# Adding a bias row to 100,000 node rows beside a sort: on GpSimd, or in 128 pieces on TensorE and ScalarE

## The reference

```python
edge_index = jnp.stack([src, dst])
h = jnp.maximum(_layernorm(x, axis=-1), 0.0)
x = x + _L0_gnn_ref(h, edge_index, L0_gnn_W, L0_gnn_att_src, L0_gnn_att_dst, L0_gnn_bias)
# ... and the same with _L1_gnn_ref, _L2_gnn_ref, _L3_gnn_ref

# inside _L0_gnn_ref
out = jax.ops.segment_sum(alpha[:, None] * h[src], dst, num_segments=N_NODES)
return jnp.tanh(out + bias)
```

## Time and profile before

| | us |
|---|---|
| three timed runs, median (lowest to highest) | 8423.18 (8384.15 to 8427.1) |
| span of the profiled execution, the only time given of it | 8526.1 |
| start of the stage with sort and node pass in that span | 42.7 |
| last instruction of the sort's network ends | 574.5 |
| last addition of the node pass ends | 709.2 |
| first instruction of layer 0 | 736.6 |

### The profile page before, as it was taken

One profiled execution on the slowest core, in us unless ns is written; L12 is line 12 of the kernel. 1 busy time (PEld: TensorE's weight loads), 2 busy tenths in 40 slices (PEclk: granted clock), 3 DMA queues, 4 the chain that ended last, 5 costly groups with the idle time before them and its releaser, 6 DMA issues. The chain is left out here.

```text
span 8526.1 us, 74303 instructions
## 1 busy us (share of the span) xinstructions
PE 4101.6 (48%) x11974; PEld 2134.1 (25%) x11974; DVE 5430.6 (64%) x9130; ACT 2417.4 (28%) x4857; POOL 5497.4 (64%) x5789
## 2 busy tenths in 40 slices
PE   0002444444466666400056666666577776666620
PEld 0000111111122222100033333433344433333310
DVE  6854777777577777699246666666544445555554
ACT  1111333333333333333023333333222222222210
POOL 5775666666566666588767777777544446666645
PEclk9999999999766666655555555555578777777765
DMA  2332222222333333377211111111122221222248
GB/s 83 98 98 74 63 63 63 64 65 57 98 93 93 93 93 93 101 216 212 51 34 40 39 41 39 40 40 39 39 62 61 62 53 40 41 40 40 41 126 249
DMA packets 846528, 647.53 MB, mean 76 GB/s; under 512 B 656112, under 2 KB 684269, under 8 KB 846271
## 3 DMA queue, kind: packets, MB, share of 16 engines
q1 hardware_dynamic: 691399, 463.53, 19.2%
q0 software_dynamic: 150560, 157.85, 8.8%
q10 hardware_dynamic: 4512, 25.60, 1.0%
HBM read 385.69 MB, written 274.56 MB: 77 GB/s over the span
## 5 line engine op out<-in xcount | busy, mean ns | idle before, releaser
L729 POOL DMA_INDIRECT l_rows<-x,l_num x1176 | 1186.5, 1009 | 461.0 <-issue 376.9
L754 POOL DMA_INDIRECT o<-l_out,l_snum x392 | 412.9, 1053 | 370.0 <-DVEq L1245 245.9
L1348 POOL DMA_INDIRECT er_edge_rows<-eat,all_perm x392 | 532.4, 1358 | 144.7 <-issue 133.8
L754 POOL DMA_INDIRECT x<-l_out,l_snum x392 | 411.3, 1049 | 305.7 <-DVEq L1095 199.6
L754 POOL DMA_INDIRECT xh<-l_out,l_snum x392 | 407.8, 1040 | 248.0 <-issue 149.5
L729 POOL DMA_INDIRECT l_rows<-in_x,l_num x392 | 444.4, 1134 | 170.4 <-issue 124.3
L754 POOL DMA_INDIRECT g<-l3b_out,l3b_snum x392 | 396.8, 1012 | 203.9 <-issue 158.1
L729 POOL DMA_INDIRECT l3b_rows<-g_rows,l3b_num x392 | 386.8, 987 | 170.8 <-issue 142.7
L729 POOL DMA_INDIRECT l3a_rows<-xh,l3a_num x392 | 383.3, 978 | 171.4 <-issue 96.9
L682 ACT ACTIVATE l_ex<-l_ex 128x1024 f32<-128x1024 f32 x294 | 310.6, 1056 | 603.5 <-DVEq L678 420.3
L949 POOL DMA_INDIRECT pre_src_rows<-in_x,all_idx_src x392 | 387.2, 988 | 141.6 <-issue 126.8
(11 more groups left out here) (368 smaller groups left out, 12553.8 us busy)
## 6 DMA issues: line engine op xcount, KB each, us to landing
l_far<-far_d SPq DMA_DIRECT2D x196, 256.0 KB
x<-ts_row SPq DMA_DIRECT2D x31, 812.5 KB
d_xrow<-x SPq DMA_DIRECT2D x31, 812.5 KB
l_far<-far_s SPq DMA_DIRECT2D x98, 256.0 KB
o<-l_fill_o SPq DMA_DIRECT2D x97, 256.0 KB
g<-l_fill SPq DMA_DIRECT2D x97, 256.0 KB
xh<-l_fill_h SPq DMA_DIRECT2D x97, 256.0 KB
ts_xin<-in_x SPq DMA_DIRECT2D x31, 800.0 KB
```

The lines of the kernel that those rows point to most:

```text
L729: pool.indirect_dma_start(self.buf[k.u][:, j, at:at + w], None, table, bass.IndirectOffsetOnAxis(ap=self.num[k.u][:, m, j:j + 1], axis=0)) ...
L754: pool.indirect_dma_start(self.table, bass.IndirectOffsetOnAxis(ap=self.num[k.u][:, j:j + 1], axis=0), self.out[k.u][:, j, 0:self.cols], N ...
L1348: pool.indirect_dma_start(c.edge_rows[:, t, :], None, eat, bass.IndirectOffsetOnAxis(ap=c.perm[:, t:t + 1], axis=0)).then_inc(c.edges_gath ...
```

## The change

GpSimd no longer adds anything. Each chunk of the node pass is cut into four pieces of 7, 6, 6 and 6 rows (448 or 384 columns), 128 pieces in all. For a piece TensorE multiplies the piece by the identity into a PSUM bank and adds, by a second product of a row of ones with the bias's tanh (now one partition of 7 copies), the bias to it. ScalarE copies the sum from PSUM to the output tile. Piece number m stands right behind level m of the sort in the streams of TensorE (behind the flip of that level, if it has one) and of ScalarE (behind the payload copy). Two PSUM banks alternate, so TensorE may be two pieces ahead of ScalarE. TensorE now waits for a chunk's load, and ScalarE for the store that frees its output buffer. SyncE's waits count pieces instead of chunks. SyncE stores the marks `far_d` and `keep_d` ahead of the node pass, for which it waits until VectorE has made them. GpSimd's stream is left with the fills and the 392 gathers.

```diff
-                beside_sync(sp)
-
                 sp.wait_ge(to_store, 1)
                 sp.dma_start(dram["far_d"].rearrange("(b p f) -> p b f", p=P, f=P), start[:]).then_inc(stored, 16)
                 sp.dma_start(dram["keep_d"].rearrange("(b p f) -> p b f", p=P, f=P), flag[:]).then_inc(stored, 16)
+
+                beside_sync(sp)
...
                     act.activation(pay[(n + 1) % 2][:], pay[n % 2][:], ACT.Copy).then_inc(pay_copied, 1)
+                    row_piece_act(act, n)
...
                         layout = need
+                    row_piece_pe(pe, m)
...
+ROW_PIECES = ((0, 7), (7, 13), (13, 19), (19, NR))
...
-    s.tb = s.sb("tb", [P, D])
+    s.tb = s.sb("tb", [1, 7, D])
+    s.p_row = [s.ps(f"p_row{u}", (P, 7 * D)) for u in range(2)]
...
+    def piece_pe(pe, m):
...
+        k = Chunk(m // per // 2, m // per % 2, c.NODE_CH)
+        lo, hi = ROW_PIECES[m % per]
+        at = s.p_row[m % 2][:, 0:(hi - lo) * D]
+        if m % per == 0:
+            pe.wait_ge(s.xin_loaded[k.u], 16 * (k.t + 1))
+        if m >= 2:
+            pe.wait_ge(s.piece_done, m - 1)
+        pe.matmul(at, c.ident[:], s.xin[k.u][:, lo:hi, :].rearrange("p r f -> p (r f)"), start=True, stop=False)
+        pe.matmul(at, c.ones_row[:], s.tb[:, 0:hi - lo, :].rearrange("p r f -> p (r f)"), start=False, stop=True).then_inc(s.piece_added, 1)
+
+    def piece_act(act, m):
...
+        if m % per == 0 and not k.first:
+            act.wait_ge(s.stored[k.u], 16 * k.t)
+        act.wait_ge(s.piece_added, m + 1)
+        act.activation(s.row[k.u][:, lo:hi, POS:POS + D], s.p_row[m % 2][:, 0:(hi - lo) * D].rearrange("p (r f) -> p r f", f=D),
+                       ACT.Copy).then_inc(s.piece_done, 1)
...
-                    sp.wait_ge(s.row_done, k.n - 2)
+                    sp.wait_ge(s.piece_done, per * (k.n - 2))
...
-        for i in range(c.NODE_CH):
...
-            pool.tensor_tensor(s.row[k.u][:, :, POS:POS + D], s.xin[k.u][:], over_rows(s.tb[0:NP, :], NR),
-                               ALU.add).then_inc(s.row_done, 1)
-            if i == 0:
-                hold(pool, c.src_known, 1)
-            for t in range(i * per, min(c.NT, (i + 1) * per)):
-                pool.indirect_dma_start(c.src_rows[:, t, :], None, x, bass.IndirectOffsetOnAxis(ap=c.idx_src[:, t:t + 1], axis=0)
-                                        ).then_inc(c.src_gathered, 16)
+        hold(pool, c.src_known, 1)
+        for t in range(c.NT):
+            pool.indirect_dma_start(c.src_rows[:, t, :], None, x, bass.IndirectOffsetOnAxis(ap=c.idx_src[:, t:t + 1], axis=0)
+                                    ).then_inc(c.src_gathered, 16)
```

More of the change, by code:

```diff
@@ L164, in prep_lists @@
     N = c.N
-    beside_act, beside_sync, beside_pool = beside
+    beside_act, beside_sync, beside_pool, row_piece_pe, row_piece_act = beside
     full, rest = E // P, E % P
@@ L905, in tables_start @@
     s.row = [s.sb(f"row{u}", [NP, NR, POS + D]) for u in range(2)]
-    s.tb = s.sb("tb", [P, D])
+    s.tb = s.sb("tb", [1, 7, D])
+    s.p_row = [s.ps(f"p_row{u}", (P, 7 * D)) for u in range(2)]
     s.xin_loaded = [s.sem(f"xin_loaded{u}") for u in range(2)]
     s.stored = [s.sem(f"stored{u}") for u in range(2)]
-    s.row_done, s.tanh_done, s.zeroed, s.ends, s.no_pos = (s.sem(n) for n in ("row_done", "tanh_done", "zeroed", "ends", "no_pos"))
+    s.piece_done, s.piece_added, s.tanh_done, s.zeroed, s.ends, s.no_pos = (
+        s.sem(n) for n in ("piece_done", "piece_added", "tanh_done", "zeroed", "ends", "no_pos"))
+    per = len(ROW_PIECES)
+    pieces = c.NODE_CH * per
     def scalar(act):
-        act.activation(s.tb[:], c.bias0[:], ACT.Tanh).then_inc(s.tanh_done, 1)
+        act.activation(s.tb[:], over_rows(c.bias0[0:1, :], 7), ACT.Tanh).then_inc(s.tanh_done, 1)
+        act.wait_ge(s.no_pos, 3)
+    def piece_pe(pe, m):
+        if m >= pieces:
+            return
+        if m == 0:
+            pe.wait_ge(s.tanh_done, 1)
+        k = Chunk(m // per // 2, m // per % 2, c.NODE_CH)
[8 more added lines that the diff above has]
+    def piece_act(act, m):
+        if m >= pieces:
+            return
+        k = Chunk(m // per // 2, m // per % 2, c.NODE_CH)
+        lo, hi = ROW_PIECES[m % per]
+        if m % per == 0 and not k.first:
[3 more added lines that the diff above has]
+                       ACT.Copy).then_inc(s.piece_done, 1)
     def sync(sp):
@@ L920, in body @@
                 if not k.first:
-                    sp.wait_ge(s.row_done, k.n - 2)
+                    sp.wait_ge(s.piece_done, per * (k.n - 2))
                 sp.dma_start(s.xin[k.u][0:node_parts(c, k)], node_rows(c, x, k)).then_inc(s.xin_loaded[k.u], 16)
             if old:
-                sp.wait_ge(s.row_done, old.n)
+                sp.wait_ge(s.piece_done, per * old.n)
                 sp.dma_start(node_rows(c, tab1, old), s.row[old.u][0:node_parts(c, old)]).then_inc(s.stored[old.u], 16)
@@ L935, in gpsimd @@
         pool.iota(c.pos[:], pattern=[[P, c.NT]], base=0, channel_multiplier=1).then_inc(s.no_pos, 1)
-        pool.wait_ge(s.no_pos, 3)
-        pool.wait_ge(s.tanh_done, 1)
-        t, per = 0, -(-c.NT // c.NODE_CH)
-        for i in range(c.NODE_CH):
[L940 to L943, removed]
-            pool.tensor_tensor(s.row[k.u][:, :, POS:POS + D], s.xin[k.u][:], over_rows(s.tb[0:NP, :], NR),
-                               ALU.add).then_inc(s.row_done, 1)
-            if i == 0:
-                hold(pool, c.src_known, 1)
-            for t in range(i * per, min(c.NT, (i + 1) * per)):
-                pool.indirect_dma_start(c.src_rows[:, t, :], None, x, bass.IndirectOffsetOnAxis(ap=c.idx_src[:, t:t + 1], axis=0)
-                                        ).then_inc(c.src_gathered, 16)
-    return scalar, sync, gpsimd
+        hold(pool, c.src_known, 1)
+        for t in range(c.NT):
+            pool.indirect_dma_start(c.src_rows[:, t, :], None, x, bass.IndirectOffsetOnAxis(ap=c.idx_src[:, t:t + 1], axis=0)
+                                    ).then_inc(c.src_gathered, 16)
+    return scalar, sync, gpsimd, piece_pe, piece_act
 class Fill:
```

## The result

| | before | after |
|---|---|---|
| timed, median (lowest to highest) | 8423.19 us (8384.15 to 8427.1, 4 runs) | 8275.98 us (8258.88 to 8300.62, 4 runs) |
| ratio of the times, 95% interval | | 0.9842 (0.981 to 0.9873) |
| span of the profiled execution | 8526.1 us | 8258.0 us |
| first and last gather start | 83.7, 704.6 | 80.5, 597.7 |
| last level of the sort starts | 572.0 | 530.5 |

The kernel became faster by 147 us of median; the forecast was a gain of 135 us, to 8288. Layer 0 starts 131 us sooner. The timeline at the end of the new first stage answers to the earlier trace rows. A row gives start and duration in us, engine, line and operation, and in brackets the idle time before it and what ended it.

The account below looks back on a forecast made before the run. The first stage was taken as bound by GpSimd's stream of gathers and additions; without additions the train ends at 599.4, plus 2.5 layer 0 starts at 602, not 736.6: gain 135 us, 8288 us, range 8250 to 8345.

Parts of the forecast that it names:

- GpSimd's additions, 103 us: GpSimd's gather train: removing 30 additions inside it, 3.44 us each, cuts it from 620.9 to 518 us.
- VectorE's stalls, 82 us, and the bare sort: Sort on VectorE: 23 stalls beside GpSimd's additions vanish, 82 us; the sort then takes 395 us and ends at 489.
- The wait of 140 us: VectorE behind the sort: its 140 us idle time goes, since the marks are stored before the node pass.
- queues passed: SyncE's queue: the sorted keys' store stays behind the node pass, which ends with level 127 of 136, so free.
- Which end is later: End of the first stage: GpSimd's gathers put layer 0 at 602, the sort would allow 511; GpSimd's is later.
- The barrier, 2.5 us: Before layer 0: 2.5 us added to the gathers' end at 599.4, so layer 0 starts at 602.
- The piece, 1.6 us: TensorE beside the sort: each of 128 pieces takes 1.6 us, under the shortest level of 2.16; cost on the path 0.
- ScalarE, 0 to 0.1 us a level: ScalarE beside the sort: 128 PSUM copies of at most 0.60 us behind the payload copies cost 0 to 0.1 us a level.
- The hand-over of a chunk, up to 14 us: Chunk loads beside the sort's first 28 levels: 0 to 2 us for each of 7 chunks, held by the cover.
- Rival D: Chunk hand-over: late loads add 9.6 us per chunk, 307 us to the sort; slower, 8504 us; chance 0.03.
- rival C: Gathers beside the sort, held by VectorE's swaps, lengthen: adds 59 us, gain 76, 8347 us; chance 0.07.
- Rival B: Sort becomes the bound through late pieces: 1.2 us more per level, gain 62 us, 8361 us; chance 0.06.

Follow-up runs that it names:

- E0: The kernel before, unchanged, timed and profiled once more: 8423.98 us, ratio to before 1.0021.
- E3: The changed kernel with only the first 8 of 128 pieces; later chunks are loaded and stored without the sum: 8302.08 us, ratio 0.9897.
- E5: The changed kernel with half of the gathers left out and all pieces but the first 8: 8208.68 us, one run.
- E1: The kernel before with only the marks' stores moved ahead of the node pass, GpSimd still adding: 8387.14 us, ratio 0.9986.
- E2: The changed kernel with the marks' stores put back behind the node pass, pieces kept: 8297.96 us, ratio 0.9864.
- E4: The changed kernel with half of the gathers left out and all pieces kept: 8231.94 us, one run.
- E8: The changed kernel again, unchanged, timed on one chip with the kernel before: 8288.71 us, ratio 0.9862.
- E6: The changed kernel with half of the gathers left out and one product per piece, the bias not added: 8160.87 us, one run.
- E9: The changed kernel with the gathers' source list built first, timed beside the changed kernel itself: 8272.85 us, ratio to before 0.9853.
- E7: The changed kernel with the gathers' source list built first, after its own five loads: 8271.37 us, ratio to before 0.9818.

## Why the prediction was right, step by step

- *GpSimd's additions, 103 us.* Right. The gathers span 597.73 - 80.54 = 517.2 us against a forecast of 518, and 620.4 in E0. The other profiles with all gathers and no additions have 513.9 to 520.6. The three pauses of the earlier trace rows stayed, at every 113th gather, with 4.4 to 5.8 us between two starts here and up to 9.3 in E3.
- *VectorE's stalls, 82 us, and the bare sort.* Right. Forecast was an end of the sort at 489 and lists that let layer 0 start at 511. E3's sort ends at 489.9, and E5's layer 0 starts at 512.1.
- *The wait of 140 us.* It goes, but not "since the marks are stored before the node pass": E1 shows that this alone moves it onto the keys' store. It goes because the pass ends beside the sort. The prediction had this second half under "queues passed", not in the removal, and credited the wrong edit.
- *Which end is later.* Right: GpSimd, in every version with all gathers.
- *The barrier, 2.5 us.* Too small. Behind the train it took 605.64 - 598.67 = 7.0 us. This is the whole error of the stage: forecast 602, measured 605.6, with the train 0.8 us shorter than forecast.
- *The piece, 1.6 us, "nothing even at 1.6".* This term was mis-sized by two. The row "x2" of the earlier trace rows was read as a pair of products; it is one float32 product in two records. The page of before says so: that line has 196 records for 98 chunks with one product each (count, busy us, mean ns).

```profile
L1297 PE MATMUL l_p_g<-l_hT,all_w_lr 128*128 128x512 f32 x196 | 200.5, 1126 | 375.3 <-DVEq L1269 373.7
```

  A piece takes about 3.15 us at 1.2 GHz for 384 columns, up to 3.66 for 448, and 1.7 at 2.4 GHz. Set against the shortest level of 2.16 us the answer would have been about 1 us for every short level at the lower clock. Measured: the sort lost 43 us in the first profile (530.5 against 487.3) and 57 to 64 in E2, E4 and E8.
- *ScalarE, 0 to 0.1 us a level.* Right for its own work (E6: no wait at all), but it passes TensorE's lateness on, 39.6 us in 45 waits.
- *The hand-over of a chunk, up to 14 us.* An upper bound that was not needed: TensorE waited 3.3 us in 3 waits for loads, and 0 to 0.8 us in E2 and E8. Rival D had no ground.
- *Gathers not slowed (rival C).* Right. From 98 to 487 us, beside the sort in every kernel, their mean is 997 ns here, 998 before and 1004 in E3, almost without pieces. The trap of the Trainium skill's page SBUF — State Buffer (section "SBUF: two separate sides") would show as a longer gather beside VectorE's copies; beside the sort's 136 levels the mean is 997 ns against 943 after them, and without the additions between the gathers it moved by less than 1%.
- *Rival B.* Its mechanism happened, at about a third of its assumed size: 0.32 to 0.47 us a level (43 to 64 us over 136) instead of 1.2. The cover of 91 us shrank to 50 (31 in E8), and would have been gone at 0.67 us a level. The forecast was right because the mis-sized term was smaller than the cover, not because it was small.
- *From the stage to the total.* 131 us in the stage, 147 between the medians. The runs of each kernel fall into two groups, seen only after the fact: before 8384 and 8423 to 8427, after 8259 and 8292 to 8301. Low against low is 125 us, high against high about 128. The rest of the 147 is which group the median came from. E8 shows it from the other side: beside it the median of before, 8387.35, fell into the lower group and E8's, 8288.71, into the upper one, so the medians stand only 99 us apart, though low against low is again 125 us and high against high 133. The stage was forecast rightly; that the difference of two medians came within 12 us of it is partly luck. The two groups go with the length of the last stage, see the end.

## What to carry to other kernels

Count the records in a row of the profile against the instructions that the code issues before taking a record, or a row, for one of them (the flips' transposes are one record each, 72 for 18 times 4, the products two): here a factor of two in the largest added cost was hidden in an "x2". When work is moved beside a serial chain, compare its slowest form with the chain's shortest step, and follow the engines that work in order between them. And when one wait has two sources in one queue, as the marks' and the keys' stores here, moving the first only shows the second.

## What the runs showed of the hardware that was not expected

- *The clock column before its first change.* It says 1.00 from the start, while until about 185 us a 384-column product takes 1.65 us, as at 1.2 GHz. In layer 0, where this part was the same work, the windows of before and of after read:

```profile
831.00:2130.00 1299.00, 566.67 (x1104) 203.31 (x1102) 975.67 (x1749) 470.51 (x1013) 854.25 (x917) 1.00 0.23 63
```

```profile
700.00:2000.00 1300.00, 566.91 (x1104) 203.41 (x1102) 976.26 (x1749) 470.37 (x1013) 853.50 (x918) 0.50 0.23 63
```

  The same 1104 records take the same time, at "1.00" and at "0.50": layer 0 ran at 1.2 GHz in both. TensorE, busy without a gap from 94 us, got the higher level at about 185 us and held it for parts of the sort only (0.66 of full speed in 300 to 400 us, 0.59 in 400 to 500). E8 had less of it (0.59 and 0.55) and its sort ended 15 us later. In E2, with the same products and as busy without a gap from 94 to 180 us, they kept the long form until about 326 us:

```profile
321.48 1.64 PE L937 MATMUL ts_p_row<-ts_tb,all_ones_row 1*128 1x384 f32 x2
...
327.36 0.91 PE L936 MATMUL ts_p_row<-ts_xin,all_ident 128*128 128x384 f32 x2
```

  Its sort ended 14 us later than in the first profile of after. So the same products are granted different clocks in different executions. What the pieces cost the sort varied too, from 43 to 64 us; that the clock makes all of this spread is not shown.

- *A barrier behind a train of gathers takes 7 us*, 6.97 to 7.05 in all six profiles taken where the gathers end last, against 2.5 where GpSimd's last gather lies far back and VectorE's list is last (E1, E4, E5, E6). It is not the transfers alone: in the changed kernel's profile the DMA engines move 6 GB/s in 600 to 602 us and nothing from 602 to 604, and layer 0 starts at 605.6. What it waits for was not tried and stays open.

- *The last stage takes 282 to 289 us or 314 to 325, once 359, with the same instructions.* Its windows, at the same place in the changed kernel's two profiles:

```profile
8050.00:8100.00 50.00, 0.00 (x0) 0.00 (x0) 21.63 (x12) 0.00 (x0) 30.94 (x6) 0.50 1.00 275
8100.00:8150.00 50.00, 0.00 (x0) 0.00 (x0) 20.25 (x12) 0.00 (x0) 30.61 (x6) 0.50 1.03 287
```

```profile
8050.00:8100.00 50.00, 0.00 (x0) 0.00 (x0) 21.64 (x9) 0.00 (x0) 17.45 (x4) 0.50 0.77 231
8100.00:8150.00 50.00, 0.00 (x0) 0.00 (x0) 23.09 (x9) 0.00 (x0) 20.37 (x5) 0.50 0.78 236
```

  The DMA engines are full at 275 to 287 GB/s in the first (8259.7 us) and at 0.77 to 0.78 with 231 to 236 in the second (8288.2 us). In the profiled executions of kernels with several runs, a short last stage goes with the lower group of times (after, E9) and a long one with the upper (E0, E1, E2, E7, E8); E3 is the exception, with 314 us in its fastest run. What makes the difference was not tried.
